# Attention outputs divided as rows of channels: transfers within on-chip memory in place of two sets of transposes

## The reference

```python
def _L1_attn_ref(x, W_key, W_query, W_value, W_proj):
    B, T, C = (4, 512, 256); NUM_HEADS = 16; HEAD_DIM = 16
    k = proj(W_key); q = proj(W_query); v = proj(W_value)      # b h t d
    scores = jnp.einsum('bhqd,bhkd->bhqk', q, k) * hd ** (-0.5)
    scores = jnp.where(causal, scores, -jnp.inf)
    weight = jax.nn.softmax(scores, axis=-1)
    out = jnp.einsum('bhqk,bhkd->bhqd', weight, v)
    out = out.transpose(0, 2, 1, 3).reshape(b, t, h * hd)
    return jnp.einsum('bto,po->btp', out, W_proj) * W_proj.shape[-1] ** (-0.5)
...
x = x + s * g          # s: the attention's output, g: silu of the experts' output
```

## Time and profile before

| | |
|---|---|
| time, median of the runs shown | 1098.3 us |
| lowest of the runs shown | 1094.94 us |
| the profiled execution's own time | 1094.69 us |
| its span in the profile | 1092.9 us |
| PE busy, share of the span | 1016.9 us, 93% |
| DVE busy, ACT busy | 501.8 us (46%), 518.9 us (47%) |
| instructions | 20884 |

### The profile page before, as it was taken

One profiled execution on the slowest core, in us unless ns is written; L12 is line 12 of the kernel. 1 busy time (PEld: TensorE's weight loads), 2 busy tenths in 40 slices (PEclk: granted clock), 3 DMA queues, 4 the chain that ended last, 5 costly groups with the idle time before them and its releaser, 6 DMA issues.

```text
span 1092.9 us, 20884 instructions
## 1 busy us (share of the span) xinstructions
PE 1016.9 (93%) x6846; PEld 701.1 (64%) x6846; DVE 501.8 (46%) x1139; ACT 518.9 (47%) x1379; POOL 192.9 (18%) x184
## 2 busy tenths in 40 slices
PE   3789999999999967989999999999999999999986
PEld 2457777777777754556666666666666656656663
DVE  4522112121121264547457467467467467466451
ACT  2424444444444524256456456456456456454443
POOL 3201001010010052131312312312313213200000
PEclk9889999999999987899999999999999999999999
DMA  6541101011012024435135145245235244224110
GB/s 198 193 136 39 48 29 58 29 39 47 29 58 106 31 86 123 70 98 146 43 131 137 45 137 127 53 135 120 65 133 111 68 140 101 68 73 112 31 40 20
DMA packets 63760, 94.22 MB, mean 86 GB/s; under 512 B 11760, under 2 KB 49136, under 8 KB 63728
## 3 DMA queue, kind: packets, MB, share of 16 engines
q1 hardware_dynamic: 57456, 89.36, 29.0%
q10 hardware_dynamic: 6272, 4.46, 1.3%
HBM read 59.94 MB, written 33.59 MB: 86 GB/s over the span
## 4 chain that ended last, share of the span: by engine, by line
PE 81%; DVE 7%; issue 3%; ACT 3%; DMA 2%; ACTq 1%; SPq 1%; POOL 0%; DVEq 0%; POOLq 0%
PE PS L768 25%; PE PS L972 7%; PE PS L874 6%; PE PS L926 6%; PE PS L907 5%; PE PS L941 5%; PE PS L840 4%; PE PS L755 4%; PE PS L819 3%; PE PS L1003 3%; DVE nm L1622 3%; PE PS L861 2%; PE PS L928 2%; PE PS L943 2%; ACTq L1236 1%
## 5 line engine op out<-in xcount | busy, mean ns | idle before, releaser
L768 PE MATMUL PS<-arena 128*128 128x256 f32 x1024 | 312.1, 421 | 0.0
L1622 DVE TENSOR_REDUCE nm<-PS 128x1 f32<-128x512 f32 (+3 forms) x352 | 207.2, 636 | 89.6 <-PE PS L928 89.5
L1293 ACT ACTIVATE arena<-PS 128x512 f32<-128x512 f32 x256 | 152.2, 600 | 168.2 <-PE PS L943 167.0
L1160 ACT ACTIVATE arena<-PS 64x8 f32<-64x8 f32 x512 | 88.5, 173 | 184.4 <-PE PS L755 180.7
L755 PEld LDWEIGHTS PS<-arena 128*72 128x72 f32 x1024 | 129.9, 141 | 68.1 <-ACT arena L1160 4.6
L768 PEld LDWEIGHTS PS<-arena 128*128 128x128 f32 x1024 | 155.5, 192 | 0.0
L941 PE MATMUL PS<-Q,K 98*128 98x512 bf16 (+3 forms) x512 | 130.9, 301 | 7.6 <-ACT arena L1293 5.6
L1478 DVE SCALAR_TENSOR_TENSOR arena<-arena 128x512 f32<-128x512 f32 x16 | 11.1, 694 | 265.7 <-ACT arena L1171 265.7
L926 PE MATMUL PS<-K,Q 96*128 96x256 bf16 (+3 forms) x512 | 121.1, 304 | 4.4 <-DMA K<-qk_d 2.5
L755 PE MATMUL PS<-arena 128*72 128x8 f32 x1024 | 121.3, 191 | 0.0
L928 PE MATMUL PS<-negmask,identb 128*128 128x128 bf16 x512 | 96.2, 222 | 0.0
(11 more groups left out here) (172 smaller groups left out, 1324.3 us busy)
## 6 DMA issues: line engine op xcount, KB each, us to landing
qk_d<-QB SPq DMA_DIRECT2D x24, 512.0 KB, 3.0
X<-in_L_attn_x SPq DMA_DIRECT2D x12, 512.0 KB, 3.5
Q<-qk_d SPq DMA_DIRECT2D x32, 192.0 KB, 4.0
K<-qk_d SPq DMA_DIRECT2D x32, 192.0 KB, 4.3
arena<-xt_d SPq DMA_DIRECT2D x16, 256.0 KB, 3.2
gt_d<-arena SPq DMA_DIRECT2D x16, 256.0 KB, 2.5
wx_d<-arena SPq DMA_DIRECT2D x16, 256.0 KB, 2.0
XT<-xt_d SPq DMA_DIRECT2D x8, 512.0 KB, 4.5
```

Of the source, the lines that this page charges most:

```text
L768: mm = pe.matmul(o, lhs, rhs, start=first, stop=last)
L1293: s_.activation(PR[:, g % 2, j, at:at + T], PS[:, bank, :], ACT.Exp, scale=SCORE_SCALE).then_inc(t_e.sem, 1)
L1622: v_.tensor_reduce(nm[:, g, h:h + n, i], PS[:, u % 3, 0:n * (i + 1) * P].rearrange("p (n w) -> p n w", n=n), AX.X, ALU.max, negate=True).t ...
```

## The change

The 15 columns of zeros in VA become ones, so that the rows 16 to 31 of each head hold the sum 16 times. After ACT's copy of a group into OS, SP issues eight transfers from OS, for each head one of the 16 rows of channels into AO and one of the 16 rows of sums into a tile DEN, both at the rows that the head's channels have in AO (`load_heads`). AO is a tile of its own now; DEN lies in HM and in a quarter of QF. DVE divides two groups at a time, k = 0 (groups 0 and 1) in stage 2 after maximum u = 8 and k = 1 (groups 2 and 3) in stage 0 of the next batch after maximum u = 10: a reciprocal in place over 128x512, then a product over 128x512. `values_turn`, `heads_turn`, `take_heads` and four small divisions are gone; `project` waits for the second `divide`.

```diff
@@ tiles @@
-        AT = sb("AT", [P, NT, D])
-        rec = sb("rec", [P, NT, NT])
+        AO = sb("AO", [P, KT, T])
...
-        AO = QF[:, 0:KT, :]
+        DEN = (HM, QF[:, 2, :])
...
+        o_ld = dcount("o_ld", 2 * H)
@@ SP @@
+            def load_heads(b, g):
+
+                sp.wait_ge(o_e.sem, o_e.at(b, g + 1))
+                k, at = g // 2, g % 2 * GH * HD
+                for h in range(GH):
+                    to = slice(at + h * HD, at + (h + 1) * HD)
+                    sp.dma_start(AO[to, k, :], OS[32 * h:32 * h + HD, :]).then_inc(o_ld.sem, 16)
+                    sp.dma_start(DEN[k][to, :], OS[32 * h + HD:32 * h + 2 * HD, :]).then_inc(o_ld.sem, 16)
+
             def stage0(b, more, first=False):
                 if not first:
+                    load_heads(b - 1, 3)
                     load_x1(b - 1, more)
                     load_operands(b, 3, True)
...
             def stage1(b, more, more2):
+                load_heads(b, 0)
                 if more2:
                     load_rows(b + 2)
                     load_gates(b + 2)
...
                 if more:
                     save_operands(b + 1, 1)
                     save_operands(b + 1, 2)
+                load_heads(b, 1)
+                if more:
                     load_operands(b + 1, 0, True)
                     load_operands(b + 1, 1, True)
...
             def stage3(b, more):
                 if more:
                     load_operands(b + 1, 2, True)
+                load_heads(b, 2)
@@ POOL @@
-            g_.memset(VA[:, :, :, :], 0.0).then_inc(f_set, 1)
-            pool.wait_ge(f_set, 1)
-            g_.memset(VA[:, :, :, HD:HD + 1], 1.0).then_inc(f_set, 1)
+            g_.memset(VA[:, :, :, :], 1.0).then_inc(f_set, 1)
@@ PE @@
-                pe.wait_ge(o_v.sem, o_v.at(b, g))
+                pe.wait_ge(o_e.sem, o_e.at(b, g))
...
-            def values_turn(b, g):
...
-            def heads_turn(b, more):
...
-            def project(b, n):
+            def project(b, n, more):
 
                 if n == 0:
-                    pe.wait_ge(r_e.sem, r_e.at(b, KT))
+                    pe.wait_ge(o_v.sem, o_v.at(b, KT))
+                if more:
+                    pe.wait_ge(s_v.sem, s_v.at(b + 2, n + 1))
+                elif more is not None:
+                    pe.wait_ge(w_e.sem, w_e.at(b + 1, NT))
@@ ACT @@
             def take_values(b, g):
                 act.wait_ge(o_mm.sem, o_mm.at(b, g + 1))
-                act.wait_ge(o_t.sem, o_t.at(b, g))
+                act.wait_ge(o_ld.sem, o_ld.at(b, 2 * GH * g))
                 s_.copy(OS[:, :], PS[:, 5, :]).then_inc(o_e.sem, 1)
-
-            def take_heads(b, ahead=1):
...
@@ DVE @@
-            def divide(b, g):
...
+            def divide(b, k):
+
+                dve.wait_ge(o_ld.sem, o_ld.at(b, H * (k + 1)))
+                v_.reciprocal(DEN[k], DEN[k]).then_inc(o_r.sem, 1)
+                dve.wait_ge(o_r.sem, o_r.at(b, k + 1))
+                v_.tensor_tensor(AO[:, k, :], AO[:, k, :], DEN[k], ALU.mult).then_inc(o_v.sem, 1)
...
-                    side = {6: [], 7: [lambda: divide(b - 1, 3)]}
+                    side = {10: [lambda: divide(b - 1, 1)]}
...
-                side = {6: [lambda: divide(b, 0)]}
+                side = {}
...
-                side = {6: [lambda: divide(b, 1)]}
+                side = {8: [lambda: divide(b, 0)]}
...
-                side = {6: [lambda: divide(b, 2)]}
+                side = {}
```

More of the change, by code:

```diff
@@ L297, in two_layers @@
         o_mm = count("o_mm", G, 2)
[L298 to L303, removed]
+        o_e = count("o_e", G)
+        o_ld = dcount("o_ld", 2 * H)
+        o_r = count("o_r", KT)
+        o_v = count("o_v", KT)
         z_mm = count("z_mm", 2, 3)
@@ L341, in _ @@
             for s in (*a_x, *a_sx, *a_ss, *c_x, c_gs, c_ws, l_xt, l_gt, l_wx, l_x, l_st, q_st, x_sv,
-                      x_ld, *q_ld, *m_ld, z_o):
+                      x_ld, *q_ld, *m_ld, o_ld, z_o):
                 sp.sem_inc(s.sem, s.credit)
@@ L523, in _ @@
             load_x1(B - 1, False)
+            stage3(B - 1, False)
+            load_heads(B - 1, 3)
             sp.wait_ge(z_o.sem, 16 * (B + 1))
@@ L1035, in stage0 @@
                         side[2].append(lambda: leave(b + 1, 1))
[L1036 to L1039, removed]
+                    side[6].append(lambda: project(b - 1, 0, more))
+                    side[7].append(lambda: project(b - 1, 1, more))
                 side[8].append(lambda: value(b, 0, first))
@@ L1044, in stage1 @@
             def stage1(b, more):
-                side = {0: [lambda: values(b, 0)], 2: [lambda: values_turn(b, 0)]}
+                side = {0: [lambda: values(b, 0)]}
                 if more:
-                    side[2].append(lambda: normal_turn(b + 1))
+                    side[2] = [lambda: normal_turn(b + 1)]
                     for n, k in enumerate((3, 4, 6, 7)):
@@ L1053, in stage2 @@
             def stage2(b, more):
-                side = {0: [lambda: values(b, 1)], 2: [lambda: values_turn(b, 1)]}
+                side = {0: [lambda: values(b, 1)]}
                 for n in range(8):
@@ L1059, in stage3 @@
             def stage3(b, more, more2):
-                side = {0: [lambda: values(b, 2)], 2: [lambda: values_turn(b, 2)]}
+                side = {0: [lambda: values(b, 2)]}
                 if more2:
                     side[1] = [lambda: mix(b + 2, 0, True)]
-                    side[2].append(lambda: mix(b + 2, 1, True))
+                    side[2] = [lambda: mix(b + 2, 1, True)]
                 if more:
@@ L1116, in _ @@
             values(B - 1, 3)
-            values_turn(B - 1, 3)
-            heads_turn(B - 1, None)
-            project(B - 1, 0)
-            project(B - 1, 1)
+            project(B - 1, 0, None)
+            project(B - 1, 1, None)
         @block.scalar
@@ L1125, in _ @@
             s_ = nc.scalar
-            for s in (a_xt, c_h, c_t, g_t, n_x2, n_xt, q_e, q_1, d_e, h_e, e_t, t_e, o_e, r_e, x_n, a_ue, g_h, m_a, n_xn,
+            for s in (a_xt, c_h, c_t, g_t, n_x2, n_xt, q_e, q_1, d_e, h_e, e_t, t_e, o_e, x_n, a_ue, g_h, m_a, n_xn,
                       w_e):
@@ L1297, in take_values @@
                 act.wait_ge(o_mm.sem, o_mm.at(b, g + 1))
-                act.wait_ge(o_t.sem, o_t.at(b, g))
+                act.wait_ge(o_ld.sem, o_ld.at(b, 2 * GH * g))
                 s_.copy(OS[:, :], PS[:, 5, :]).then_inc(o_e.sem, 1)
-            def take_heads(b, ahead=1):
-                act.wait_ge(q_2.sem, q_2.at(b + ahead, 2))
-                for k in range(KT):
-                    act.wait_ge(r_t.sem, r_t.at(b, k + 1))
-                    s_.copy(AO[:, k], PS[:, 6 + k, :]).then_inc(r_e.sem, 1)
             def store(b):
@@ L1329, in stage0 @@
                     side[1] = [lambda: take_values(b - 1, 3)]
-                    side[4] = [lambda: take_heads(b - 1)]
                 stage(b, 0, side)
@@ L1415, in _ @@
             take_values(B - 1, 3)
-            take_heads(B - 1, 0)
             store(B - 1)
@@ L1529, in remainder @@
                 if n == 0:
-                    dve.wait_ge(z_mm.sem, z_mm.at(b - 1, 0))
                     dve.wait_ge(q_1.sem, q_1.at(b, 0))
@@ L1712, in stage3 @@
             def stage3(b, more, more2):
-                side = {6: [lambda: divide(b, 2)]}
+                side = {}
                 if more2:
                     side[4] = [lambda: mixed(b + 2, 0)]
-                    side[6].insert(0, lambda: mixed(b + 2, 1))
+                    side[6] = [lambda: mixed(b + 2, 1)]
                 if more:
@@ L1762, in _ @@
             choose(0)
-            dve.wait_ge(f_set, 2)
+            dve.wait_ge(f_set, 1)
             stage({}, (0, 0))
@@ L1783, in _ @@
             stage3(B - 1, False, False)
-            divide(B - 1, 3)
+            divide(B - 1, 1)
             finish(B - 1, 0)
```

25 lines of the change are left out of this document (1 added, 24 removed).

## The result

The changed kernel takes 1223.2 us (median) beside 1097.3 us before: a ratio of 1.112, with a 95% interval of 1.109 to 1.116. It is slower, as forecast, but by 126 us where the prediction adds 58 to the profiled execution's 1094.7 us (a ratio of 1.053), and outside its range of 1105 to 1175. Each ratio has its own runs of the kernel before beside it, whose medians go from 1097.3 to 1100.9 us. The profiled execution of the changed kernel has a span of 1222.1 us, that of before 1092.9.

The account below looks back on a forecast made before the run. PE's own list was taken as the bound. On 1094.7 us: stage 0 +18.9, stage 2 +18.9 and +2.0, stages 1 and 3 -7.0, end +5.9, making 1133; the falling clock adds 20, giving 1153 us, range 1105 to 1175.

Parts of the forecast that it names:

- Stage 0: PE idles 3.5 us before `project` and loses 2.7 us, seven times; the half clock behind it adds 20 us in all.
- Stage 3: No division there; it keeps the transposes' gain of 0.44 us a batch.
- Stage 1's gain of 0.44 us: No division in stage 1, so PE keeps 0.44 us a batch from the removed transposes.
- What SP does behind them ... moves back by 3.6 us. Those are needed a stage or more later, and I cost that at nothing: SP's loads and operands queued behind the eight transfers of a group go out 3.6 us later, at no cost.
- Two plain loads are issued 0.45 us apart: SP's issue step for the eight transfers of a group, so the eighth starts 3.2 us after the first.
- I leave the clock up there: Stage 2: PE's 2.4 us wait before the turn of the maxima was taken not to lower the granted clock.
- the rival with the clock falling in stage 2: The clock falls in stage 2 as well: eight times 2.2 us, +18, giving 1171 us; chance 0.22.
- The end: After the last copy, eight issues, landing and division make the last `project` start 5.9 us later.
- late transfers: Rival: the sums land 4.1 us after issue in stages 2, 0 and the end, 23 us more, 1176 us; chance 0.03.
- the prediction's two rows: PE idle times before the loop: 2.18 us left the granted clock at 1.00, 2.53 us was followed by half clock.

Follow-up runs that it names:

- The fill: Changed kernel with seven matmuls of no use on PE before the projection in stage 0 and seven before the turn of the maxima in stage 2: 1188.9 us.
- the fill with 14 and 12: Changed kernel with 14 matmuls of no use before the projection in stage 0 and 12 before the turn of the maxima in stage 2: 1209.3 us.

## Why the prediction was right about the sign and wrong about the size

The difference between the two spans is 129.2 us: 6.9 in the start, and by stages, all eight batches, +18.6 (stage 1), +55.2 (stage 2), -2.9 (stage 3), +40.6 (stage 0), +10.9 (end). The forecast of 1153 us is -3.5, +20.9, -3.5, +38.9 (with the clock) and +5.9.

- **Stage 0 was right in its mechanism and its total.** The wait (3.70 us), the product as its releaser and the half clock behind it are there. The run without the reciprocal and the one with the late projection both end at 20.8 us. In the parts the sizes shift: the clock is 2.25 us, not 2.9, in a steady batch, and the last stage 0, which has less work of PE to cover the division, loses 9.5 us (27.3 for 17.8), where the forecast takes the same 5.6 for each. The total is nearer than its parts: what the steady batches lose less and the last one more nearly cancel.
- **Stage 3 was right** (-0.4 us). **Stage 1's gain of 0.44 us is not there** even without the collision: 19.7 us before and after. In both kernels PE waits 0.28 us in it for DVE's remainders ahead of the distances; the chain of queries and keys appears to set that stage and not PE's list. That was read from the rows, not tried.
- **"What SP does behind them ... moves back by 3.6 us. Those are needed a stage or more later, and I cost that at nothing"** is the step that failed. They are indeed needed later. But SP's list stands at the wait for ACT's copy ahead of the eight issues, so the large loads move by 7 us and not by 3.6; and the loads do not have to be needed to cost: they fill the transfer engines just when ACT's two small transfers, on which PE waits, are issued. The prediction asked who waits for the late loads and not whom they meet. The run with the loads first puts it at 3.2 us in stage 1 and 0.6 in stage 2, 3.8 us a batch. The Trainium skill (DMA: Bandwidth & Descriptors, "Issuing engines are not separate DMA queues") says that transfers of ACT and SP end up on the same 16 engines and interleave; the trace agrees, with 5.9 us for 4 KB at 333 GB/s.
- **"Two plain loads are issued 0.45 us apart"** was the wrong row. The transfers' step is 0.62 us. The trace of before has such a step too, in the operands that SP issues in stage 2:

```profile
741.72 0.59 SPq L468 DMA_DIRECT2D K<-qk_d  x1
742.36 0.59 SPq L468 DMA_DIRECT2D Q<-qk_d  x1
```

  Eight of them take 1.2 us more than the sum has, so the sums of stage 2 land later and PE waits 3.43 us there (with the loads first) and not 2.4.
- **"I leave the clock up there"** in stage 2 fell with it. In the run with the loads first the turn of the maxima comes 15.6 us after the stage's first `values`, where it was 12.4 us before, 3.2 late; from there to the next `values` PE needs 8.6 us for 5.8, without another wait, at a granted clock of 0.50 over the first 5.5 us. The fill divides the 2.8 us: with the clock up it is 6.5 to 6.7, so 2.0 us are the clock's and 0.8 the late low maxima, which the forecast has. That is the rival with the clock falling in stage 2, to which 0.22 was given, with 2.0 us for its 2.2. One wait bears this out without any fill. In the run with the projection late, the first turn of the maxima waits as long, but the granted clock stays at 1.00. Timeline of PE, and then a stretch (columns as in the earlier trace rows):

```profile
511.32 0.28 PE L947 MATMUL PS<-ident,nm 128*16 128x128 f32 x1 [3.77 <-DVE nm L1604]
```

```profile
511.32:514.32 3.00, 3.00 (x18) 2.37 (x18) 2.52 (x21) 0.85 (x2) 0.94 (x1) 1.00 0.98 180
```

  From there to the next `values` it is 6.5 us. So a steady stage 2 of the changed kernel, 6.6 us longer than before, is 0.6 at its head, after the wait that the late loads make; 3.2 for the late turn, where the forecast has 1.9; 2.0 for the clock; 0.8 for the low maxima.
- **The end** was mis-sized by 5 us. The issue takes 1.0 more, the rest is the half clock in which PE does the last `values` (4.50 us for 2.36) and the projection (5.39 for 3.72), which the forecast did not follow into PE's last work. The projection stands behind 11.14 us of idle time; ahead of the last `values` PE has only waits of up to 0.7 us, as before the change, where the clock stayed up, and what brought it down there stays open.

Of the 70 us between forecast and profile, 34 are stage 2, 22 stage 1, 5 the end, 7 the start and 2 stage 0. The step on SP's queue was costed at nothing and is the one that no rival had: a chance of 0.03 stood for late transfers, as a matter of the eight transfers and not of those behind them.

## What to carry to other kernels

Where a step puts transfers into an ordered queue, price what is queued behind it by its new time of issue, wait at the head included, and look which small, urgent transfer of another engine then meets it; being needed late is no excuse. A long operation off the bound engine is free or dear by its place: 3.35 us on DVE cost PE 5.4 us behind the last maximum and next to nothing where PE had two other steps to do first. When one wait is taken away, look for the next at the same place before calling the theory wrong.

## What the hardware showed besides

The length of a wait did not foretell the clock here. The loop's first `values` waits 2.18 or 2.19 us in eight of these runs, behind the same steps of PE. Over the next 3 us the granted clock was 1.00 in two of them (the kernel before, and the fill with 14 and 12) and 0.62 to 0.67 in the six others, the changed kernel among them. Stretches, before and after (columns as in the earlier trace rows):

```profile
472.98:475.98 3.00, 3.00 (x39) 1.46 (x40) 1.73 (x3) 2.24 (x5) 0.37 (x2) 1.00 0.00 0
479.84:482.84 3.00, 3.00 (x24) 1.15 (x28) 1.74 (x3) 2.07 (x4) 0.38 (x2) 0.64 0.00 0
```

A wait of 1.46 us in the fill with 14 and 12 was followed by 0.50 over 3 us, the one of 3.77 us shown above by 1.00. So the prediction's two rows, 2.18 us at full clock and 2.53 us at half, mark no border between them, and "I leave the clock up there" had less to stand on than it seemed. What decides it these runs do not show.

The late loads also made DVE slower, in a place that hardly counts here. Timelines of DVE and POOL, at the end of stage 1 after:

```profile
786.14 4.50 DVE L1520 TENSOR_TENSOR QB<-QF,QB 128x1024 bf16<-128x1024 f32 x2
786.62 2.94 POOL L626 TENSOR_TENSOR WX<-WX,UC 128x1024 f32<-128x1024 f32 x1 [22.93 <-DMA WX<-wx_d]
```

and of DVE at the same step with the large loads first:

```profile
770.99 2.42 DVE L1520 TENSOR_TENSOR QB<-QF,QB 128x1024 bf16<-128x1024 f32 x2
```

POOL's addition, which the late load released, ran together with two subtractions of DVE: 4.50 us for 2.42, and 2.94 for the 2.35 that it takes with the loads first. The times come near to operations that shut each other out: the first subtraction ends at 787.36, the addition 2.20 us later at 789.56, the second subtraction 1.08 us after that, and alone these two take 2.35 and 1.22. In all six batches in which they meet, the second subtraction takes 3.30 to 3.31 us. The Trainium skill (SBUF — State Buffer, "Who interferes with whom") says that an operation of DVE with two inputs in SBUF contends with one of GpSimd that reads SBUF, and that such contention is an exclusive lock; the trace agrees with 2.08 us lost on DVE.
